# Graph attention with residual norm on one core: the low half of the attention on GpSimd, later stores, another fill and drain

## What is computed

```python
q = (x @ Wq.T).reshape(b, n, 12, 32)
k = (x @ Wk.T).reshape(b, n, 12, 32)
v = (x @ Wv.T + bv).reshape(b, n, 12, 32)
scores = einsum('bqhd,bkhd->bhqk', q, k) * scale + (adj + adj)[:, None]
row_nonzero = any(scores != 0, axis=-1, keepdims=True)
p = nan_to_num(softmax(where(row_nonzero, scores, -inf), axis=-1))
out = einsum('bhqk,bkhd->bqhd', p, v).reshape(b, n, 384)
return layernorm(x + out @ Wo.T + bo)        # no gain, no shift, all f32
```

## Time and profile before

| what | value |
|---|---|
| median of 3 runs (lowest, highest) | 601.19 us (601.16, 602.58) |
| profiled execution, its own time | 600.63 us |
| its span from first to last instruction | 598.8 us |
| mean granted TensorE clock | 0.998 |
| busy: PE, DVE, ACT, POOL | 97%, 83%, 83%, 71% |
| chain that ended last | PE 85%, DMA 5%, ACT 5%, DVE 4% |

### The profile page before, as it was taken

One profiled execution on the slowest core, in us unless ns is written; L12 is line 12 of the kernel. 1 busy time (PEld: TensorE's weight loads), 2 busy tenths in 40 slices (PEclk: granted clock), 3 DMA queues, 4 the chain that ended last, 5 costly groups with the idle time before them and its releaser, 6 DMA issues.

```text
span 598.8 us, 23532 instructions
## 1 busy us (share of the span) xinstructions
PE 580.2 (97%) x8448; PEld 510.6 (85%) x8448; DVE 495.5 (83%) x2380; ACT 497.2 (83%) x1975; POOL 425.2 (71%) x691
## 2 busy tenths in 40 slices
PE   8989999999999999999999999999999999999785
PEld 5778888888988898888888888888888888988664
DVE  4678888888888888888888888888888888888885
ACT  5697988988888988888888888988888888887983
POOL 0686867877686786777777686786777777665772
PEclk9999999999999999999999999999999999999999
DMA  8411423223243242323223242242324222122221
GB/s 304 162 39 32 129 91 95 102 93 105 85 131 92 65 146 79 110 91 117 79 92 110 79 131 93 65 144 69 120 91 126 75 88 83 53 92 81 89 84 67
DMA packets 34749, 59.62 MB, mean 100 GB/s; under 512 B 10569, under 2 KB 24009, under 8 KB 34633
## 3 DMA queue, kind: packets, MB, share of 16 engines
q1 hardware_dynamic: 34200, 57.53, 30.0%
q10 hardware_dynamic: 432, 0.59, 0.3%
HBM read 44.50 MB, written 13.62 MB: 97 GB/s over the span
## 4 chain that ended last, share of the span: by engine, by line
PE 85%; DMA 5%; ACT 5%; DVE 4%; issue 1%; SPq 0%; POOLq 0%; DVEq 0%; POOL 0%
PE qk_ps L346 30%; PE scores_ps L439 15%; PE v_ps L382 14%; PE scores_ps L369 8%; PE scores_ps L422 8%; PE qk_ps L399 7%; ACT probs L492 4%; DMA scale_t<-scale_mem 2%; DMA scale_mem<-scale_rows 2%; DVE nscores L591 2%; PE scores_ps L451 1%; DMA nscores<-wk 1%; PE spare_ps L399 1%; PE v_ps L451 0%; PE qk_ps L451 0%
## 5 line engine op out<-in xcount | busy, mean ns | idle before, releaser
L492 ACT ACTIVATE probs<-nscores,neg_max 128x128 f32<-128x128 f32 x768 | 297.3, 389 | 8.3 <-DVE neg_max L591 3.7
L591 DVE CUSTOM_DVE_ANT_0 nscores<-scores_ps,adj_n 128x128 f32<-128x128 f32 x768 | 171.5, 285 | 27.8 <-PE scores_ps L369 27.8
L289 POOL TENSOR_TENSOR tree<-nscores 128x256 f32<-128x256 f32 x192 | 143.3, 746 | 17.3 <-DVE neg_max L591 17.3
L492 ACT ACTIVATION_READ_ACCUMULATOR probs<-nscores,neg_max 128x1 f32 x768 | 144.3, 188 | 0.0
L517 ACT ACTIVATE probs_t<-qk_ps 128x384 f32<-128x384 f32 (+1 forms) x128 | 63.0, 493 | 75.1 <-PE spare_ps L399 72.5
L439 PE MATMUL scores_ps<-w_o,att_t 128*128 128x384 f32 x576 | 112.3, 339 | 4.7 <-DVE neg_max L591 3.0
L382 PE MATMUL v_ps<-w_v,x_t 128*128 128x384 f32 x576 | 111.5, 338 | 3.1 <-ACT probs_t L517 3.1
L289 POOL TENSOR_TENSOR tree<-tree 128x128 f32<-128x128 f32 x192 | 102.4, 533 | 15.1
L382 PEld LDWEIGHTS v_ps<-w_v,x_t 128*128 128x128 f32 x576 | 101.8, 188 | 9.3 <-ACT probs_t L517 4.0
L346 PE MATMUL qk_ps<-x_t,w_q 128*128 128x512 f32 (+1 forms) x540 | 107.4, 343 | 0.6 <-ACT probs_t L517 0.6
L346 PE MATMUL qk_ps<-x_t,w_k 128*128 128x512 f32 (+1 forms) x540 | 107.2, 343 | 0.0
(11 more groups left out here) (71 smaller groups left out, 921.5 us busy)
## 6 DMA issues: line engine op xcount, KB each, us to landing
x_n<-xn SPq DMA_DIRECT2D x32, 384.0 KB, 5.0
scale_t<-scale_mem SPq DMA_DIRECT2D x63, 192.0 KB
out<-out_n SPq DMA_DIRECT2D x31, 384.0 KB, 2.6
x_raw<-xt SPq DMA_DIRECT2D x15, 768.0 KB, 5.7
adj_n<-adj SPq DMA_DIRECT2D x32, 128.0 KB, 4.5
scale_mem<-scale_rows SPq DMA_DIRECT2D x63, 16.0 KB
x_raw<-xt SPq DMA_DIRECT2D x3, 256.0 KB, 4.9
nscores<-wq ACTq DMA_DIRECT2D x3, 192.0 KB, 4.3
```

The source lines that it names most:

```text
L289: nc.gpsimd.tensor_tensor(tree[:, b % 2, low:high, 0:width], src[:, :, 0:width], src[:, :, width:2 * width], ALU.add).then_inc(tree_step, 1)
L492: last = nc.scalar.activation(probs[:, b % 2, h], nscores[:, b % 2, h], ACT.Exp, bias=neg_max[:, b % 2, h:h + 1], scale=-1.0, accum_out=ro ...
L591: last = nc.vector.tensor_tensor_reduce(out=nscores[:, half, h], in0=scores_ps[j][:, m * P:(m + 1) * P], in1=adj_n[:, b // 2 % 2, half], s ...
```

## The change

`attention_low(b)` for graphs 0 to 60 leaves DVE's slots and stands first in POOL's (the last three graphs stay with DVE); `project_out` now waits for `att_split` too. The low half of w_o moves from DVE to POOL. Stores move from odd SP steps to behind the scale's DMAs of the next even step. Two splits of group 2 leave slots -2 and -1 for slots 0 and 1. PE's first group starts with the high products of k-tile 0 alone. The last query tile is kept in two pieces. ACT makes w_o's high half between two key tiles. In slots without projection and in the drain `keep_turned_high` stands ahead of `find_scale`. The last graph's values go to another bank, so that `values(63)` doesn't wait for ACT, and DVE takes two of that graph's turned banks instead of one.

```diff
+        def value_bank(b):
+            return scores_ps[2] if direct(b) else v_ps
+        def lows(b):
+            return LOWS - 1 if direct(b) else LOWS
...
             g, k = (b + 2) // GRP + 2, (b + 2) % GRP
+            if g == 2:
+                return {0: ((g, 0), (g, 1)), 1: ((g, 2),)}.get(b, ())
             return ((g, k),) if k < KT and g < NG else ()
...
+            def store(pair):
+                sp.wait_ge(out_ready, 2 * pair + 2)
+                sp.dma_start(out[pair], out_n[:, pair % 2]).then_inc(stored[pair % 2], DMA)
...
-                        sp.wait_ge(out_ready, b - 1)
-                        sp.dma_start(out[pair - 1], out_n[:, (pair - 1) % 2]).then_inc(stored[(pair - 1) % 2], DMA)
+                elif b >= 4:
+                    store(b // 2 - 2)
...
+            pool.wait_ge(w_high, 2)
+            nc.gpsimd.tensor_tensor(w_o[:, LO], raw_o, w_o[:, HI].bitcast(F32), ALU.subtract).then_inc(wo_split, 1)
             pool.wait_ge(bias_in, 2 * DMA)
+            def attention_low(b):
+                pool.wait_ge(att_high, b + 1)
+                nc.gpsimd.tensor_tensor(att_t[:, b % 2, LO].rearrange("p m q -> p (m q)"), att_n[:, b % 2],
+                                        att_t[:, b % 2, HI].rearrange("p m q -> p (m q)").bitcast(F32),
+                                        ALU.subtract).then_inc(att_split, 1)
             for b in range(-2, NB + 2):
+                if has(b - 1) and b < NB - 2:
+                    attention_low(b - 1)
                 if has(b - 2):
                     find_rstd(b - 2)
...
-                pe.wait_ge(v_ready, b + 1)
+                if not direct(b):
+                    pe.wait_ge(v_ready, b + 1)
...
             def project_out(b):
+                pe.wait_ge(att_split, b + 1)
                 if has(b + 3):
                     pe.wait_ge(biased, KT * (b + 4))
...
+            for t in range(TILES):
+                if t < 2:
+                    pe.wait_ge(first_high, t + 2)
+                project_first(0, t, TERMS[:1])
+            pe.wait_ge(first_split, 3)
+            for t in range(TILES):
+                project_first(0, t, TERMS[1:])
...
-            act.wait_ge(wo_in, DMA)
-            nc.scalar.activation(w_o[:, HI], raw_o, ACT.Copy).then_inc(w_high, 1)
+                if m == 0:
+                    act.wait_ge(wo_in, DMA)
+                    nc.scalar.activation(w_o[:, HI], raw_o, ACT.Copy).then_inc(w_high, 1)
...
-            keep_turned_low(NB - 2, 1, 0, 2)
+            keep_turned_low(NB - 2, 0, 1, 2)
             attention_high(NB - 3)
-            keep_turned_low(NB - 1, 0, 1, 2)
             attention_high(NB - 2)
+            keep_turned_low(NB - 1, 0, 1)
             attention_high(NB - 1)
...
+                for cols in ((slice(0, GRP * P),) if m < KT - 1 else (slice(0, P), slice(P, GRP * P))):
+                    nc.vector.tensor_scalar(q_t[:, 0, m, cols], first_ps[2 * m + 1][:, cols], 0.5 * SCALE, None,
+                                            ALU.mult).then_inc(first_queries, 1)
...
                 bias_and_max(b + 2, 1)
-                if has(b - 1):
-                    attention_low(b - 1)
                 bias_and_max(b + 2, 2)
+                if has(b) and not projected(b):
+                    keep_turned_high(b)
                 if has(b + 1):
                     find_scale(b + 1)
-                if has(b):
-                    keep_turned_high(b)
                 if projected(b):
+                    if has(b):
+                        keep_turned_high(b)
                     keep_first(b)
-                if b == -2:
-                    split_w_low(1, w_o, raw_o)
...
             find_scale(NB - 1)
+            attention_low(NB - 3)
             keep_v(NB - 1)
-            attention_low(NB - 3)
+            normalise(NB - 2)
+            keep_turned_high(NB - 1)
             moments(NB - 4)
-            keep_turned_high(NB - 1)
-            normalise(NB - 2)
+            attention_low(NB - 2)
             residual(NB - 3)
-            attention_low(NB - 2)
             normalise(NB - 1)
```

More of the change, by code:

```diff
@@ L242, in _ @@
                         sp.dma_start(adj_n[:, pair % 2], adj[pair + 2]).then_inc(adj_in[pair % 2], DMA)
[L243 to L248 removed]
+                    if 1 <= pair < NB // 2 - 1:
+                        sp.wait_ge(y_ready, b - 1)
+                        sp.dma_start(x_n[:, (pair + 1) % 2], xn[pair + 1]).then_inc(xn_in[(pair + 1) % 2], DMA)
+                elif b >= 4:
+                    store(b // 2 - 2)
                 if b % GRP == GRP - 1 and b // GRP + 4 < NG:
@@ L253, in _ @@
             last = NB // 2 - 1
+            store(last - 1)
             for half in range(2):
@@ L431, in project_out @@
                 else:
-                    pe.wait_ge(att_split, b + 1)
                     if not has(b + 1):
@@ L614, in keep_turned_high @@
                 wait(dve, pv_done, b)
-                for j in range(LOWS, HPT):
+                for j in range(lows(b), HPT):
                     nc.vector.tensor_copy(turned_rows(b, j), turned_bank(b, j)).then_inc(turned_high, 1)
```

54 lines of the change are left out of this document (25 added, 29 removed).

## The result

| | before | after |
|---|---|---|
| median of 4 runs each (lowest, highest) | 601.17 us (600.4, 602.58) | 595.83 us (594.82, 596.85) |
| profiled execution | 600.63 us, span 598.8 | 596.39 us, span 594.6 |

The ratio is 0.9908, 95% interval 0.9882 to 0.9935: faster by 5.3 us, where 5.8 had been forecast. The four runs stand in two pairs: 594.82 and 595.26 at a mean granted clock of 0.998 and 1.000, and 596.39 and 596.85 at 0.997.

The account below looks back on a forecast made before the run. PE, busy 97% of the span, was taken as the bound, leaving gains mostly in fill and drain. Fill 2.0, middle 1.3 and drain 2.5 sum to 5.8 us: 594.8 profiled, 595.4 as run median, range 594.0 to 598.0.

Parts of the forecast that it names:

- Step (1): Fill: PE starts with the high products of k-tile 0 instead of idling for the low halves; 0.6 us won.
- last rival: Drain's loop held by something beside the low half, fill's start by PE's warm-up; gain 2.7 us, 598.5; chance 0.04.
- (2): Fill: first scores wait for only 128 columns of the last query tile; 0.4 us won.
- Step (3): Fill: two splits of x taken out of ACT's gapless stretch from 22.77 to 33.7 us; 1.0 us won.
- I take the full 1.3: Middle: moving stores behind the scale removes DVE's waits for it, winning all 1.3 us available between slots 3 and 57.
- return 4.53: Drain's end: the way back of graph 62's scale was taken to last 4.53 us, as in the kernel before.
- The new order puts more behind it: Drain's end: ACT's turned copies of graph 63 now stand behind `attention_high(62)`; two wide copies, 1.1 us.
- Half: Rival: fill or drain gives half as ACT becomes the bound; gain 3.5 us, 597.7; chance 0.14.
- Stalls stay or move: Rival: x_raw, x_n and adj leave together and may meet the scale's next write; 596.7 us; chance 0.08.
- POOL holds DVE: Rival: each added POOL pass blocks DVE for 1.02 us, costing 4 us over four drain slots; 599.4; chance 0.04.
- Overflow: Rival: POOL's low half exceeds 2.6 us in steady slots, so PE waits for `att_split`; 606 at 2.8 us; chance 0.03.
- last sign of a wrong prediction: Fill: the prediction would be wrong if ACT runs without any gap in slots 0 and 1.

Follow-up runs that it names:

- e5: The changed kernel with graph 63's turned banks copied ahead of graph 62's normalise and high half, which wait for the scale; 593.39 us, ratio 0.9879.
- e7: The changed kernel with the one store behind graph 62's scale held back until that scale has landed; 593.69 us, ratio 0.9882.
- e4: The changed kernel with the splits of group 2 back in slots -2 to 0; 597.53 us, ratio 0.9941.
- e3: The changed kernel with the attention's low half back on DVE in the slots, all else changed; 597.45 us, ratio 0.9947.
- e1: The kernel before with only the low half of graphs 0 to 60 moved to POOL; 602.73 us, ratio 1.0018.
- e9: The kernel before with the low half on POOL and the stores behind the scale, old fill and drain lists; 595.78 us, ratio 0.9919.
- e10: The changed kernel with graph 63's turned banks first, last store held back, two idle products at PE's start, one split fewer in slot 0; 593.13 us, ratio 0.9881.
- e8: The changed kernel with two in place of three idle products of zeros ahead of PE's first product; 594.19 us, ratio 0.9896.
- e2: The kernel before with only the stores moved behind the scale of the next even step; 597.42 us, ratio 0.995.
- e12: The changed kernel with POOL finding each low half of graphs 0 to 60 three times; 663.1 us (one run).

## Why the prediction held, step by step

**Time.** Forecast 595.4 [594.0, 598.0] and faster; measured 595.83. The parts were less right than the sum. By the profiled execution, forecast 2.0, 1.3 and 2.5 for fill, middle and drain; measured 1.35, 1.9 and 1.0.

**Fill, forecast 2.0.** Measured 1.35. Step (1), 0.6 for PE's earlier start, gave 0.27 in the profiled execution (PE's first group ended at 19.54 for 19.81). The prediction named the reason in its last rival: PE's own warm-up holds the start. In after the first real product still runs at a slow pace (1.26 us at 5.93), and the second stands at 7.03; with the same code it stands at 6.50, 6.33 and 6.08 in e5 to e7, so after is the slow end of this step. With steps (1) and (2) together the first exponential starts at 21.1 to 22.1 in the eight executions that have both and three idle products, and at 22.4 to 22.8 in the four that have neither: 1.1 in the mean, where 1.0 was forecast. Step (3) is the term that was mis-sized: 1.0 forecast, 0.7 measured (11.96 less 11.27 in before and after, 0.65 by e4). The 1.0 is there at slot 0's projection, where the step was read. But the exponentials of slot 0 then wait for DVE's bias passes of graph 2, and those for its scores. PE makes the scores behind the second key tile, and only one of the two splits stood ahead of that tile. So the next bound was not the split moved into slot 0 ("0.5 fits, barely"), but a path that the sum didn't follow. Other executions with this fill reach slot 3 at 57.2 to 57.5, against 58.0 in after and 59.0 to 59.3 in the old fill with the clock up, so 1.0 to 2.1 us are won.

**Middle, low half, forecast 0.** Held, by e3's 481.5 and by e1, whose steady slots are no shorter. The cover was named rightly, but the edit was costed without asking what a faster DVE triggers: e1 has 11 scale waits for five.

**Middle, stores, forecast 1.3.** Measured 1.9. The term "I take the full 1.3" was mis-sized by 0.6. The waits are gone, as forecast; the rest is the pace of an undisturbed slot, 8.917 us in after against 8.928. With e9 and e10 at 8.933, under the same middle, this is how executions differ and not the change: 0.6 of this stage is luck.

**Drain slots, forecast 2.0.** Measured 2.4, the upper end: 4 x 0.48 for the low half and 4 x 0.13 for `keep_turned_high`, by the square of e1 and e3. The forecast had the 0.5 of both in one and left the second at nothing. ACT is now busy for 7.00 of 7.08 us in slots 59 to 61, as "next in line is ACT" said.

**Drain, the end, forecast 0.5 won.** Measured 1.35 lost: here a step failed. The write took 1.95 us where 2.0 was said, and the scale came back at 581.33. The forecast's 584.4 counts neither fill nor middle; less their 3.3 it is 581.1, and the slots had won 0.4 more than forecast. Missing from it is the store: "return 4.53" had none right behind it and took 5.11 with one, 0.6 us. What followed the return took 13.3 us in place of 12. "The new order puts more behind it" was seen and priced rightly: two wide copies at 1.1 us, which did take 1.0 (582.45 to 583.46), and in e8, where the clock held, 12.1 us from the return (580.28) to the end of the span. Not in the sum was the clock, 1.2 us, which no row of before pointed to in the drain. Nor was the alternative: in e5 the same copies are done before the scale is back, and the end is 1.4 us better than e8's. The stores alone shorten the end by 1.3 us (e2); the new order gives that back, and the clock took another 1.2.

That the total came within 0.5 us of the forecast is partly luck: the middle and the drain's slots gave 1.0 us more than forecast, the fill and the end 2.5 less, and the median of the runs gained 1.1 us more than the profiled execution did.

**The rivals.** *Half*: its 597.7 did not come. ACT is the bound in slot 0 and in the drain's slots, but not by the split. *Stalls stay or move*: refuted by e2, where DVE never waits for the scale. *POOL holds DVE*: in the slots no; 768 bias passes keep a mean of 0.29 us (285 ns before, 287 after). In the drain once, by another pass of POOL. Two timelines of the changed kernel, DVE and POOL:

```profile
578.05 1.31 DVE L706 TENSOR_TENSOR att_t<-att_n,att_t 128x384 fp32r<-128x384 f32 x1
```

```profile
576.00 2.95 POOL L294 TENSOR_TENSOR x_n<-x_n,bo_rows 128x384 f32<-128x384 f32 x3
```

DVE's low half of graph 61, two operands in SBUF, takes 1.31 us in place of 0.55 and ends 0.4 us after POOL's third addition has, at 579.36 and 578.95. That is the case that the Trainium skill, SBUF — State Buffer, section Who interferes with whom, names, and the trace agrees; its other half agrees too: the bias passes, with PSUM as one source, run at 0.29 beside POOL. The warning of the Trainium skill, Perfetto Trace Analysis, section Optimizing Scalar/DVE Operations, that offloading between the two might not help, does not hold for this pass: POOL runs it in 1.02 us, DVE is free of it, and POOL's small tree pass, 533, 533 and 527 ns in the mean where DVE has the low half (before, e2, e3), falls to 465, 470 and 469 where POOL has it (after, e1, e9). *Overflow*: the mechanism is real (e12), its threshold was put too high, 2.6 for 1.9 to 2.0 us, because POOL's busy share leaves out the gaps between its instructions. The wait for its first operand, 1.03 us a slot, would have given 1.02 + 1.03 = 2.05.

**The signs.** POOL is busy for 80% where 79% was said, its low half takes 1.02 us for 1.0, the drain's slots 7.08 for 7.2, and PE never waits for `att_split` in a slot. Late against the forecast are the exponentials (22.11 for 21.8), slot 0's projection (32.48 for 32.1) and slot 3's (58.06 for 57.4); the scale of graph 62 is back 13.3 us before the end of the span where 12 was said. ACT has 0.20 us idle in slot 0 and 1.66 in slot 1, so the last sign of a wrong prediction didn't appear either.

**What stays open.** What decides in which execution the clock falls; why slots take 8.933 us in some executions and 8.917 in others; why e1 has more waits for the scale; and whether e10 is better than e5: 593.13 and 593.39 have overlapping intervals. Both beat the kernel before. Their runs (592.77 to 594.33) also lie below all four of the changed kernel (594.82 to 596.85), but the intervals of the ratios overlap slightly (up to 0.9900, from 0.9882), so that rests on the stages: e5's end is 2.6 us shorter than after's, by two lines moved.

## What to carry to other kernels

Parts of a change needn't add: the low half alone won nothing (1.0018), the stores alone 3.5 us, both 4.8. The shorter slots paid only once the scale's round trip no longer stood in their way. Before a copy is put behind a wait for a transfer, ask who else is behind it in that engine's list, and measure an engine's room by the wait ahead of its first operand, not by its busy share. Where one kernel's runs fall into two groups, look at the granted clock of the ends before explaining the difference by the code.

## What the runs showed of the hardware

**The clock in short stretches.** In some executions the granted clock goes to 0.50 for 2 to 4 us in the fill (e1 from 34 us, e4 from 33) or in the drain (after, e1, e3, e4, e12), in others of nearly the same code never. The 24 matmuls of `attend` took 1.45 us in after, where the fall came at their start, and 0.86 otherwise; the last 18 matmuls took 4.40 to 4.99 us with the fall and 3.49 to 3.84 without. PE's idle time just ahead doesn't tell the cases apart: the clock fell after 2.16 us (after), 2.34 (e3) and 1.81 (e4), and did not after 2.07 (e8). In e2 the runs at a mean clock of 0.994 or 0.995 took 598.77 to 598.82 us and those at 0.997 to 1.000 took 597.1 to 597.44.

**Small writes behind big transfers.** In the drain the 16 KB write of the scale takes 1.94 or 1.95 us with nothing right ahead, and 2.25 behind a store; in the middle it takes 4.2 to 4.9 behind a store and an x of four graphs (e1's chain). The 192 KB back take 4.02 to 4.53 us with nothing issued behind them (e7, before) and 4.76 to 5.29 with a store issued 0.6 us behind. A later transfer thus slows an earlier one.
